# An expert layer's row tiles: turned by way of a DRAM scratch and VectorE's 32x32 blocks in place of TensorE's identity products

## What is computed

```
x = x + autocorrelation(layernorm(x), ctx, ctx)        # 8 heads, by spectra, top 12 lags
n = layernorm(x)                                       # no scale, no shift
gate = top-16 softmax of (n @ Wq.T) @ keys.T           # 64 experts
z = n @ A.T                                            # 512 = 64 experts x rank 8
x = x + 2 * ((z * gate) @ B.T)
```

## Time and profile before

| | |
|---|---|
| median of 3 runs | 2156.32 us (2156.14 to 2157.71) |
| profiled execution | 2156.57 us |
| its span | 2154.8 us |
| instructions | 29239 |
| DMA, whole span | 287.5 MB, mean 133 GB/s, 38.3% of 16 engines |
| one step of the expert stage | 25.33 us |

### The profile page before, as it was taken

The page is one execution under the profiler, slowest core; times in us unless marked ns, Lnnn a source line. Parts: engine busy times, 40 slices in busy tenths (PEclk is TensorE's granted clock), DMA queues, the critical chain, the costliest instruction groups (busy, mean ns, idle before and its releaser), DMA issues.

```text
span 2154.8 us, 29239 instructions
## 1 busy us (share of the span) xinstructions
PE 2115.7 (98%) x8920; PEld 1328.0 (62%) x8920; DVE 1673.8 (78%) x4051; ACT 1337.5 (62%) x3051; POOL 1561.3 (72%) x965
## 2 busy tenths in 40 slices
PE   5999999999999999999999999999999999999999
PEld 2455455455455455454454454888888888888887
DVE  7999999999999999999999999644444444444443
ACT  4786786786786786786765646644444455445441
POOL 6999999999999999999999988633343433333420
PEclk9999999999999999999999999999999999999999
DMA  7232333333333332333221246544545444444431
GB/s 282 97 108 103 120 111 103 120 111 103 121 109 103 121 109 103 122 109 103 103 89 64 83 168 239 171 158 166 175 164 174 159 166 165 158 166 172 164 119 59
DMA packets 110705, 287.50 MB, mean 133 GB/s; under 512 B 7168, under 2 KB 7296, under 8 KB 109568
## 3 DMA queue, kind: packets, MB, share of 16 engines
q1 hardware_dynamic: 110592, 286.19, 38.3%
HBM read 219.06 MB, written 67.11 MB: 133 GB/s over the span
## 4 chain that ended last, share of the span: by engine, by line
PE 82%; DVE 7%; POOL 6%; ACT 2%; issue 2%; DMA 1%; SPq 0%; DVEq 0%; ACTq 0%; POOLq 0%
PE pair L755 11%; PE pair L749 8%; PE out L581 6%; PE out L582 6%; PE out L583 6%; PE z L583 5%; PE z L582 5%; PE z L581 5%; PE pair L644 5%; PE evac L631 4%; PE evac L655 4%; PE evac L656 4%; PE lag L698 4%; PE pair L745 4%; PE tp L600 2%; POOL r_f L1804 2%
## 5 line engine op out<-in xcount | busy, mean ns | idle before, releaser
L1838 POOL TENSOR_TENSOR rows<-rows,cin 128x1024 f32<-128x1024 f32 x48 | 117.0, 2437 | 325.7 <-DMA rows<-out_dram 273.6
L755 PE MATMUL pair<-r_f,back 128*128 128x512 f32 x768 | 342.7, 597 | 0.5 <-DVE prod L1035 0.5
L1804 POOL TENSOR_TENSOR r_f<-prod 128x1024 f32<-128x1024 f32 x128 | 303.0, 2378 | 9.3 <-DVE prod L1033 7.4
L755 PEld LDWEIGHTS pair<-r_f,back 128*128 128x128 f32 x768 | 143.0, 190 | 192.7 <-issue 146.5
L749 PE MATMUL pair<-w_sb,wts 128*128 128x512 f32 x512 | 225.1, 592 | 1.4 <-ACT w_sb L1625 0.9
L1480 ACT ACTIVATE xn<-tp 128x512 f32<-128x512 f32 x94 | 55.1, 586 | 231.0 <-PE tp L600 230.9
L581 PE MATMUL z<-a_hi,xt 128*128 128x512 f32 x496 | 195.9, 395 | 0.0
L581 PE MATMUL out<-b_hi,zt_hi 128*128 128x512 f32 x492 | 194.3, 395 | 0.0
L583 PE MATMUL z<-a_hi,xt 128*128 128x512 f32 x496 | 193.4, 390 | 0.0
L582 PE MATMUL z<-a_lo,xt 128*128 128x512 f32 x496 | 193.3, 390 | 0.0
L582 PE MATMUL out<-b_lo,zt_hi 128*128 128x512 f32 x492 | 191.6, 389 | 0.0
(11 more groups left out here) (234 smaller groups left out, 5576.8 us busy)
## 6 DMA issues: line engine op xcount, KB each, us to landing
out_dram<-att_sb SPq DMA_DIRECT2D x32, 1024.0 KB, 4.2
rows<-out_dram SPq DMA_DIRECT2D x64, 512.0 KB, 3.8
cin<-out_dram SPq DMA_DIRECT2D x63, 512.0 KB, 4.0
xin<-in_x_dram SPq DMA_DIRECT2D x63, 512.0 KB, 4.1
vf<-in_ctx_dram SPq DMA_DIRECT2D x31, 1024.0 KB, 5.1
out_dram<-rows SPq DMA_DIRECT2D x62, 512.0 KB, 2.8
xf<-in_x_dram SPq DMA_DIRECT2D x30, 1024.0 KB, 5.3
stat_in<-in_x_dram SPq DMA_DIRECT2D x27, 1024.0 KB, 5.1
```

Of the source, the lines that this page charges most:

```text
L755: return nc.tensor.matmul(pair_ps[:, bank, :], back[:, 3 * bank + n, :], r_f[:, row, :], start=n == 0, stop=n == 2)
L1804: nc.gpsimd.tensor_tensor(dst, prod[:, slot, 0:2, :], prod[:, slot, 2:4, :], ALU.add).then_inc(add_done, 1)
L1838: nc.gpsimd.tensor_tensor(half, first, other, op).then_inc(c_added, 1)
```

## The change

For tiles from 3 on (`FIRST_SPREAD`), TensorE no longer turns the normalized rows. ScalarE writes them to `xn` in two halves of 128x1024; half h holds, for each of four parts b of a row, 256 numbers. SyncE stores each half to a DRAM scratch (512 KB) and, when the store has landed, loads it back with four DMAs, one for each b: part b of row 32c + j goes to partition 32b + j, in the c-th quarter of the columns. VectorE then turns every 32x32 block of a half in place of its partitions and columns, straight into the four PSUM banks, two instructions for each half. The feature that ends on partition p of block k is now another one than before, so the host lays A and Wq out to match, and tiles 0 to 2, still turned by TensorE, are normalized into `xn` in the matching order of columns.

In the order of the engines: SyncE's stores stand first in its step, its loads after `load_rows` of half 1 and before `load_others`; VectorE's turning stands between `zt_low` and `route`; ScalarE's copy of a quarter waits until its whole half is turned, since the copy overwrites `xn`; TensorE goes from the scores straight to the output, with waits for the turned z.

```diff
--- before.py
+++ after.py
@@ -247,6 +247,10 @@
         x2_added, stat2_step, root2_done, norm2_ready = (
             sem("x2_added"), sem("stat2_step"), sem("root2_done"), sem("norm2_ready"))
         xn_ready, tp_ready = sem("xn_ready"), sem("tp_ready")
+        xn_half = sem("xn_half")
+        turn_stored = [sem(f"turn_stored{h}") for h in range(2)]
+        turn_loaded = [sem(f"turn_loaded{h}") for h in range(2)]
+        turn_rows = nc.dram_tensor("turn_rows", (2, P, D // 2), F32, kind="Internal").ap()
         tp_hi, tp_lo, tp_full = sem("tp_hi"), sem("tp_lo"), sem("tp_full")
         q_ready, q_copied, sc_ready, sc_copied = sem("q_ready"), sem("q_copied"), sem("sc_ready"), sem("sc_copied")
         route_step, gate_exp, gate_step, gate_ready = (
@@ -383,6 +387,12 @@
         def turned_z(u, low):
 
             return xt[:, low, 0:KN, :] if is_step(u, TT) else (zt_lo if low else zt_hi)[:]
+
+        FIRST_SPREAD = 3
+        SPREAD = P // 4
+
+        def spread(t):
+            return not (isinstance(t, int) and t < FIRST_SPREAD)
 
         def later_tile(u):
             return not (isinstance(u, int) and u + 2 >= TT)
@@ -553,10 +563,29 @@
 
             steps(body)
 
+            def store_turn(t, h):
+
+                sp.wait_ge(xn_half, 2 * (t - FIRST_SPREAD) + h + 1)
+                sp.dma_start(turn_rows[h], xn[:, h * (D // 2):(h + 1) * (D // 2)]).then_inc(turn_stored[h], 16)
+
+            def load_turn(t, h):
+
+                sp.wait_ge(turn_stored[h], 16 * (t - FIRST_SPREAD + 1))
+                from_rows = turn_rows[h].rearrange("(c j) (b f) -> b j c f", c=4, b=4)
+                to = xn[:, h * (D // 2):(h + 1) * (D // 2)].rearrange("p (c f) -> p c f", c=4)
+                for b in range(4):
+                    sp.dma_start(to[SPREAD * b:SPREAD * (b + 1)], from_rows[b]).then_inc(turn_loaded[h], 16)
+
             def tile_step(u, k, r, a, b, f):
+                if f and spread(u + 1):
+                    for h in range(2):
+                        store_turn(u + 1, h)
                 if later_tile(u) and not (isinstance(u, int) and u < 2):
                     sp.wait_ge(out_stored, 16 * (2 * u - 2))
                     load_rows(k, 3 + r, 1)
+                if f and spread(u + 1):
+                    for h in range(2):
+                        load_turn(u + 1, h)
                 if later_tile(u) and b:
                     load_others(k, 3 + r, 1)
                 if later_tile(u + 1):
@@ -891,11 +920,11 @@
                                         b_hi[:, q, m, :], b_lo[:, q, m, :], m == 0, m == KN - 1)
                     last.then_inc(out_ready, 1)
 
-                if f and not is_step(u, 0):
+                if f and not (is_step(u, 0) or spread(u + 1)):
                     for q in range(4):
                         turn_tile(u + 1, q)
                 if b:
-                    if not f:
+                    if not f or spread(u + 1):
                         pe.wait_ge(zt_hi_done, u)
                         pe.wait_ge(zt_lo_done, u)
                     for q in range(4):
@@ -994,6 +1023,16 @@
                 part = slice(4 * q, 4 * q + 4)
                 nc.vector.tensor_tensor(xt[:, 1, part, :], tp_ps[bank_of(t, q)][:], xt[:, 0, part, :].bitcast(F32),
                                         ALU.subtract).then_inc(tp_lo, 1)
+
+            def turn_spread(t, q):
+
+                h, g = q // 2, q % 2
+                if g == 0:
+                    dve.wait_ge(turn_loaded[h], 64 * (t - FIRST_SPREAD + 1))
+                if q == 3:
+                    dve.wait_ge(zt_lo_done, t - 1)
+                by_block = xn[:].rearrange("p (h c g m i) -> p h g m c i", h=2, c=4, g=2, m=4)[:, h, g]
+                nc.vector.transpose(tp_ps[q][:].rearrange("p m (c j) -> p m c j", c=4), by_block).then_inc(tp_ready, 1)
 
             def half_statistics(t, slot, h):
                 dve.wait_ge(x2_added, 2 * t + h + 1)
@@ -1359,6 +1398,9 @@
                     return
                 if not is_step(u, TT):
                     zt_low()
+                if f and spread(u + 1):
+                    for q in range(4):
+                        turn_spread(u + 1, q)
                 if a:
                     route()
                 if f:
@@ -1476,7 +1518,7 @@
 
             def tile_high(t, q):
                 n = tp_at(t, q)
-                act.wait_ge(tp_ready, n + 1)
+                act.wait_ge(tp_ready, n + 2 - q % 2 if spread(t) else n + 1)
                 nc.scalar.activation(xt_full[:, q, :, :], tp_ps[bank_of(t, q)][:], ACT.Copy).then_inc(tp_full, 1)
                 act.wait_ge(tp_full, n + 1)
                 nc.scalar.activation(xt[:, 0, 4 * q:4 * q + 4, :], xt_full[:, q, :, :], ACT.Copy).then_inc(tp_hi, 1)
@@ -1506,8 +1548,15 @@
 
             def norm_rows(t, slot):
                 act.wait_ge(norm2_ready, 2 * t + 2)
-                nc.scalar.activation(xn[:], rows[slot][:], ACT.Identity, bias=shift2[:],
-                                     scale=rstd2[:]).then_inc(xn_ready, 1)
+                if spread(t):
+                    for h in range(2):
+                        nc.scalar.activation(xn[:].rearrange("p (h b f) -> p h b f", h=2, b=4)[:, h],
+                                             rows[slot][:].rearrange("p (b h f) -> p h b f", h=2, b=4)[:, h],
+                                             ACT.Identity, bias=shift2[:], scale=rstd2[:]).then_inc(xn_half, 1)
+                else:
+                    nc.scalar.activation(xn[:].rearrange("p (k b i) -> p b k i", b=4, k=KD),
+                                         rows[slot][:].rearrange("p (b k i) -> p b k i", b=4, k=KD),
+                                         ACT.Identity, bias=shift2[:], scale=rstd2[:]).then_inc(xn_ready, 1)
 
             act.wait_ge(consts_set, 2)
             nc.scalar.activation(inv_sum[:, 0:1], consts[:, 1:2], ACT.Sqrt)
@@ -1957,12 +2006,12 @@
     if name in _INS[:2]:
         return a[:, ROWS, :]
     if name == "L0_ffn_A_w":
-        return a.reshape(NFFN, 4, 4, P).transpose(1, 3, 2, 0).reshape(4, P, D)
+        return a.reshape(NFFN, 4, 4, 4, P // 4).transpose(2, 1, 4, 3, 0).reshape(4, P, D)
     if name == "L0_ffn_B_w":
         return a.reshape(4, 512, KN, P).transpose(0, 3, 2, 1).reshape(4, P, D)
     if name == "L0_ffn_Wq_w":
         wide = np.zeros((P, KD, 32), a.dtype)
-        wide[:, :, :RDIM] = a.reshape(RDIM, KD, P).transpose(2, 1, 0)
+        wide[:, :, :RDIM] = a.reshape(RDIM, 4, KD, P // 4).transpose(1, 3, 2, 0).reshape(P, KD, RDIM)
         return wide.reshape(P, KD * 32)
     tall = np.zeros((4, 32, EXPERTS), a.dtype)
     tall[:, :RDIM] = a.T
```

## The result

| | before | after |
|---|---|---|
| median | 2157.02 us | 2284.22 us (2280.42 to 2290.72) |
| span of the profiled execution | 2154.8 us | 2285.7 us |
| one step of the expert stage | 25.33 us | 29.87 us, mean of 20 (28.3 to 31.1) |
| copy of the scores, us behind the first z matmul of its step | +11.36 | about +17.0 (15.7 to 18.3) |

The change is slower: ratio 1.0593, 95% interval 1.0581 to 1.0606. The forecast said slower, but 2170, in a range that ended at 2195. The 29 changed steps are longer by 4.4 us on average (the last of them, with no loads of later tiles beside it, is shorter), and that is all but 2 us of the 131 us between the two spans.

A forecast was written before the change was run, and what follows sets the result against it. TensorE's stream, busy 98% of the span, was taken as the bound. A 2.1 us wait less 1.63 saved is 0.47 a step, 13.7 over 29: 2156.57 + 13.7 = 2170 us, range 2120 to 2195.

The forecast's parts named there:

- The products, 1.63 us a step: TensorE's 16 identity products of the next tile go away, saving 1.63 us a step, 47.3 us at most over 29.
- Short runs of the layout, ScalarE's two halves, VectorE's 0.62 for a turn: Normalization writes in runs of 32 cost nothing; ScalarE's halves end near +2.4 and +3.5; each VectorE turn instruction takes 0.62 us.
- rival 3: VectorE's turn instructions bound the step at 1.25 us each, +1.7 us a step, 2206 us; chance 0.08 with Rival 4.
- Issues at +2.5, +4.05, +5.3 to +8.55: SyncE's issue times from a step's first z matmul: first store, load of the rows' other half, eight quarter loads.
- The price of a turned half, 2.5 us: Four narrow loads from the scratch take 2.5 us a half, so halves land at +10.5 and +13.0.
- the row load landed at +8.0: SyncE's 512 KB load of the rows' other half, behind a store still under way, lands about +8.0.
- T: When VectorE's queue is free for route and the score copy, from the step's first z matmul; forecast +14.25, before +11.36.
- my lower end, 1.3: Lowest price considered for loading a turned half: 1.3 us, from queued 512 KB loads landing 1.2 to 1.3 us apart.
- T + 7.3 for the second add: VectorE's work from route to the end of the second output add takes 7.3 us, ending at +21.55.
- The wait at the fourth quarter: TensorE wants the fourth output quarter at +19.45 and waits 2.1 us for VectorE's second add.
- The clock at 1.00: TensorE's granted clock stays at 1.00, 2.4 GHz, despite waits of 2 us in 26; nothing added.
- Rival 4: Loading a turned half costs 3.8 us, T = +16.85, a loss of 3.07 us a step, 2246 us; 0.08 with rival 3.

The follow-up runs named there:

- direct: The change without the store to and load from DRAM scratch; VectorE turns ScalarE's output directly, exchange between partitions left out: 2119.84 us, ratio 0.983.
- turn_first: The change with the loads of the turned halves issued ahead of the load of the rows' second half in SyncE's queue: 2290.39 us, ratio 1.0612.
- whole: The change with each half loaded back by one DMA over 128 partitions in 4 KB pieces, exchange between partitions left out: 2213.99 us, ratio 1.0263.
- wide1k: The change with four loads a half over 128 partitions each, in 1 KB pieces, exchange between partitions left out: 2237.94 us, ratio 1.0374.
- gate_psum: The change with the gate's intermediate product written to and read from PSUM in place of SBUF: 2257.82 us, ratio 1.0472.
- half_wide: The change with the gate in PSUM and only half 0 through DRAM, by four stores and one load over 128 partitions; TensorE turns half 1: 2244.65 us.
- both other orders: Turned halves' loads ahead of the rows' second-half load, against the change: 2290.39 us; first-half load moved behind too, gate in PSUM: 2277.99 us.

## Why the prediction was wrong

By its own steps:

- *The products, 1.63 us a step*: right. `direct` gains 1.3 a step, with 0.3 lost at the fourth quarter.
- *Short runs of the layout, ScalarE's two halves, VectorE's 0.62 for a turn*: right or near. The layout costs 0, the halves take 2.38 for 2.10, a pair of turns 1.23 to 1.25 as forecast; with `direct`, rival 3 has fallen.
- *Issues at +2.5, +4.05, +5.3 to +8.55*: right, to 0.4 us.
- *The price of a turned half, 2.5 us, and the row load landed at +8.0*: **this step failed**. I let the transfers land one behind the other, each with its own price, as three loads seemed to do in the earlier trace rows. They shared the engines. The packets show it, counted from the first quarter load (1809.17) to the landing of the first half (1816.97), and from there to the landing of the second (1819.85). Those between 512 B and 2 KB are the pieces of the turned halves, 1024 for both; those under 512 B carry next to no bytes:

```profile
DMA packets 1311, 1.85 MB, mean 237 GB/s; under 512 B 145, under 2 KB 1097, under 8 KB 1311
...
DMA packets 250, 0.70 MB, mean 242 GB/s; under 512 B 26, under 2 KB 98, under 8 KB 250
```

  When the first half landed, 1097 - 145 = 952 of the 1024 pieces of both halves had gone: the second half had not stood behind it but had run beside it, and the row load before. The last 72 then went beside 152 larger packets, of the partner and input loads, which were issued after +9. The engines were busy throughout. So the row load landed at +10.7 and the halves at +13.0 and +15.9. A half did come 2.9 after the other; it was the first that was 2.5 late. `turn_first` shows the part of the row load: with it behind them the same halves landed at +9.9 and +12.2.

  How much of the 2.8 us by which T was late is which? Had I priced wide halves at my lower end, 1.3, my own working would have put T of `whole` at 8.0 + 2.6 + 1.25 = +11.85. It was +14.1, so some 2.3 come from the sharing, narrow or not: whole halves took 6.1 to 6.4 us, and the row load 6.0. The narrow form measured 2.9 (17.0 against 14.1), where I had charged 2.4 for it; that is the other 0.5. What the Trainium skill says in "SBUF — State Buffer", section "Door 1: The DMA port swizzle", that 32 partitions reach half of the ports and hold a transfer near 218 GB/s, is in line with the 224 GB/s at full share, against 323 in `wide1k`; but its ratio gave me a price for a narrow load by itself, and not for what else is under way with it.
- *T + 7.3 for the second add*: wrong by 0.8 in the step shown (1829.15 - 1821.08 = 8.07), by 1.1 in `whole`. The gate operation is held by GpSimd's late add. I had moved that add to +14.5, saw that it delays no one who reads it, and did not ask what VectorE does at the same time. With the gate out of its way (`gate_psum`) the second add ends at T and 7.1. The gate is 26 us of the whole.
- *The wait at the fourth quarter*: at the third instead, in the step shown, and in most other steps at the third and then at the fourth too (0.1 to 2.1 us). With T at +17.1 the first add, T and 3.2, comes after the third quarter is wanted (+16.9). The forecast's T would have had both.
- *The clock at 1.00*: wrong. Behind 3.56 us of idle it was 0.50 for a quarter, which took 5.28 us. The wait of 2.12 us in `whole` left it at 1.00 in three steps of four.

The sum again, for the step shown. The forecast had 25.80. T is 2.9 later, the second add another 0.8 behind it: 29.5. The clock adds the 0.5 worked out above: 30.0, and the step has 30.17. Over all steps (29.87) the 4.1 us of the miss divide alike: 2.8 for the landings, 0.8 for the gate, 0.5 for the clock. Rival 4, which had T at +16.85, gave 2246: the path and most of the size stood in the text, with 0.08 for it and rival 3 together. Its mechanism was still the wrong one, a dearer price for each half in turn, because I read the earlier trace rows as a queue and not as three transfers that share the engines. The direction, slower, was forecast by a margin of 14 us against 127; that it came true says little for the working.

What stays open: how the 94 us of the way through DRAM at full width divide between the landing of the halves and the ring's other links; why a turned store lands later behind a row load and an output store; and why the small stores of `half_wide` keep only some four engines busy.

## What to carry to other kernels

Price a new transfer with all that is under way beside it: add up the bytes from the first issue to the landing that counts, divide by the rate that a trace shows for such a crowd, and take that as the latest landing. For the change this gives 2.6 MB (row load, two halves, partner, input) at 216 to 254 GB/s, 10 to 12 us behind +4.3, and the second half landed 11.6 behind it. It is an upper bound: in `turn_first` the same sum gives +15 or later, and the halves, with the row load behind them, landed by +12.2. In a ring of load, compute and store, ask before you reorder a queue which link the moved transfer feeds: here both other orders moved the delay and neither removed it. And when a helper engine's work moves in time, look at what the others execute at its new place, not only at who reads its result.

## What was not expected of the hardware

- VectorE's 128x64 operations with SBUF on both sides took 1.27 (TENSOR_SCALAR) and up to 2.46 us (TENSOR_TENSOR) in place of 0.25 and 0.23 while GpSimd added in SBUF; with the result in PSUM 0.29.
- VectorE's turn of 128x512 float32 in 32x32 blocks into PSUM: 0.68 to 0.73 us, 0.64 apart.
- TensorE's granted clock at 0.50 for some 5 us behind 3.56 us of idle, and this cost nothing where the next wait was longer.
- A store of 512 KB landed after 2.7 us, and after 5.8 where a load and another store had been issued in the 1.7 us before it.
- Four stores of 128 KB in pieces of 1 KB landed some 6 us after the last issue, with a row load beside them, where one store of 512 KB took 2.7; with little else left to move, the 16 engines were 26% busy at 75 GB/s.
- At the same full share, the 16 engines moved 323 GB/s with loads to 128 partitions and 224 with loads to 32.
